# Band scratch laid out with four heads side by side, and a new table of step times, in a two-thread fused kernel

## The reference, cut to what matters

```
for l in 0..3:
    xn = layernorm(x);  s = attn_l(xn);  g = silu(ffn_l(xn));  x = x + s * g
```

```
weights = softmax(logits over 32 offsets)            # [b, head, t, offset]
out[b, head, t, :] = sum_o weights[b, head, t, o] * value[b, head, t - 31 + o, :]
```

## Time and profile before

| | us |
|---|---|
| median of 3 executions | 3785.52 (3783.11 to 3786.83) |
| the profiled execution | 3781.06 |
| its span, first to last instruction | 3779.3 |
| TensorE busy | 3062.2 (81% of the span) |
| VectorE busy | 2423.9 (64%) |
| ScalarE busy | 1666.3 (44%) |
| GpSimd busy | 597.1 (16%) |
| mean granted TensorE clock | 0.884 of full speed |

### The profile page before, as it was taken

The page is one execution under the profiler, slowest core; times in us unless marked ns, Lnnn a source line. Parts: engine busy times, 40 slices in busy tenths (PEclk is TensorE's granted clock), DMA queues, the critical chain, the costliest instruction groups (busy, mean ns, idle before and its releaser), DMA issues.

```text
span 3779.3 us, 43414 instructions
## 1 busy us (share of the span) xinstructions
PE 3062.2 (81%) x15958; PEld 1536.6 (41%) x16050; DVE 2423.9 (64%) x4577; ACT 1666.3 (44%) x2467; POOL 597.1 (16%) x425
## 2 busy tenths in 40 slices
PE   5468869997799868998589976998679986898579
PEld 1124423553245432554235532454325542355225
DVE  7435876568756775668755686557765687552635
ACT  5314615464245534456154652456344561542143
POOL 2001101311023010321013110230103210130113
PEclk7568869998799979998899987999799987998799
DMA  3530275312842066502753028420565127531344
GB/s 114 62 111 9 53 137 135 104 26 74 141 145 69 21 112 131 151 28 53 136 135 104 24 73 143 144 72 20 111 119 161 32 51 139 131 105 36 75 131 126
DMA packets 331157, 353.80 MB, mean 94 GB/s; under 512 B 98433, under 2 KB 264129, under 8 KB 329345
## 3 DMA queue, kind: packets, MB, share of 16 engines
q1 hardware_dynamic: 330945, 351.02, 40.2%
HBM read 301.70 MB, written 48.61 MB: 93 GB/s over the span
## 4 chain that ended last, share of the span: by engine, by line
PE 52%; DVE 28%; DMA 6%; ACT 5%; issue 5%; POOL 2%; SPq 2%; ACTq 0%; DVEq 0%; POOLq 0%
DVE MX L1613 7%; PE PS L1824 6%; PE PS L1847 6%; PE PS L1851 5%; PE PS L1678 5%; PE PS L1686 5%; PE PS L1111 3%; DVE U L897 3%; PE PS L1792 3%; DMA UU<-k_scratch 3%; DVE U L904 3%; PE PS L1803 2%; DVE D L1667 2%; DVE D L956 1%; POOL D L1419 1%
## 5 line engine op out<-in xcount | busy, mean ns | idle before, releaser
L1419 POOL TENSOR_TENSOR D<-D,GW 128x512 f32<-128x512 f32 x320 | 435.1, 1361 | 1412.6 <-ACT D L1492 1177.5
L787 ACT ACTIVATE U<-U 128x2048 f32<-128x2048 f32 x256 | 487.9, 1909 | 180.5 <-DVE U L897 98.4
L1662 DVE SCALAR_TENSOR_TENSOR D<-D,PS 128x512 f32<-128x512 f32 x336 | 229.0, 681 | 402.3 <-ACT D L1496 284.6
L1492 ACT ACTIVATE D<-PS 128x512 f32<-128x512 f32 x336 | 200.0, 595 | 614.8 <-PE PS L1847 614.8
L1824 PEld LDWEIGHTS PS<-WST,D 128*128 128x128 f32 (+1 forms) x2688 | 354.6, 199 | 165.3 <-DVE D L1667 95.5
L1824 PE MATMUL PS<-WST,D 128*128 128x128 f32 (+1 forms) x2688 | 381.9, 287 | 30.5 <-DVE D L1667 30.5
L1851 PE MATMUL PS<-XT,WST 128*128 128x512 f32 (+1 forms) x672 | 373.3, 638 | 27.4 <-DVE D L1662 26.0
L904 DVE SCALAR_TENSOR_TENSOR U<-PP,RD,QB 128x512 f32<-128x512 f32 x512 | 361.8, 772 | 47.5 <-ACT QB L784 28.7
L1111 PE MATMUL PS<-U,resident 128*32 128x512 f32 x2048 | 303.7, 673 | 102.5 <-ACT U L787 102.5
L1847 PE MATMUL PS<-XT,WST 128*128 128x512 f32 (+1 forms) x672 | 370.2, 634 | 8.5 <-DMA WST<-in_pairs_dram 4.3
L1613 DVE TENSOR_REDUCE MX<-PS 128x2 f32<-128x1024 f32 x256 | 297.9, 1219 | 88.1 <-PE PS L1770 88.1
(11 more groups left out here) (356 smaller groups left out, 3822.0 us busy)
## 6 DMA issues: line engine op xcount, KB each, us to landing
GW<-gates_scratch SPq DMA_DIRECT2D x320, 256.0 KB, 4.4
WST<-in_pairs_dram SPq DMA_DIRECT2D x336, 192.0 KB, 2.4
U<-band_scratch SPq DMA_DIRECT2D x32, 1280.0 KB, 15.3
UU<-in_w_dram SPq DMA_DIRECT2D x64, 512.0 KB, 7.2
UU<-pad_scratch SPq DMA_DIRECT2D x8, 1792.0 KB
UU<-q_scratch SPq DMA_DIRECT2D x24, 384.0 KB
UU<-k_scratch SPq DMA_DIRECT2D x24, 384.0 KB
e_scratch<-D SPq DMA_DIRECT2D x8, 1024.0 KB, 4.5
```

The source lines that it names most:

```text
L787: e.activation(ring(i), ring(i), ACT.Gelu).then_inc(S["act"], 1)
L1419: e.tensor_tensor(AV[:, n % 3, :], AV[:, n % 3, :], GW[:, p // 2 % GWS, p % 2, :], ALU.mult).then_inc(S["gated"], 1)
```

## The change

It has two parts.

**Layout.** `band_scratch` becomes `(NT, NH/4, P, 4*BAND)`: the bands of four heads lie interleaved, element by element, in one matrix of 640 columns. A store's run is 32 offsets of 4 heads (128 floats, 512 bytes), a load's run is 640 floats (2560 bytes), four per partition where 16 were. The bytes are the same. `WBT` takes the same order, so ScalarE's copy L803 becomes two activations of half the size (one per half of the heads). L1164 reads a head's band at a step of four floats.

```diff
-        z_dram = nc.dram_tensor("band_scratch", (NT, NH, P, BAND), FP32).ap()
+        z_dram = nc.dram_tensor("band_scratch", (NT, NH // 4, P, 4 * BAND), FP32).ap()
...
-                dst = bass.AP(z_dram.tensor, j * NH * P * BAND, [[BAND + 1, P], [P * BAND, NH], [1, HOR]])
-                e.dma_start(dst, WBT[:, j, :, :]).then_inc(S[f"z_stored{j}"], 16)
+                dst = bass.AP(z_dram.tensor, j * NH * P * BAND, [[4 * BAND + 4, P], [4 * P * BAND, NH // 4], [1, 4 * HOR]])
+                e.dma_start(dst, WBT[:, j].rearrange("p g o r -> p g (o r)")).then_inc(S[f"z_stored{j}"], 16)
...
-                e.dma_start(band(j), z_dram[j].rearrange("n p t -> p n t")).then_inc(S[f"band{j}"], 16)
+                e.dma_start(band(j).rearrange("p g t r -> p g (t r)"), z_dram[j].rearrange("g p t -> p g t")).then_inc(S[f"band{j}"], 16)
...
-                src = PS(j).rearrange("p (h o n) -> p h n o", h=2, o=HOR)
-                e.activation(WBT[:, j, :, :].rearrange("p (h n) o -> p h n o", h=2), src, ACT.Copy).then_inc(S["soft_act"], 1)
+                for h in range(2):
+                    src = PS(j)[:, 256 * h:256 * h + 256].rearrange("p (o g r) -> p g o r", o=HOR, g=2)
+                    last = e.activation(WBT[:, j, 2 * h:2 * h + 2], src, ACT.Copy)
+                last.then_inc(S["soft_act"], 1)
...
-                                            band(j)[:, 8 * h + 2 * q + r, 0:w], start=(j == 0 and r == 0),
+                                            band(j)[:, 2 * h + q // 2, 0:w, 2 * (q % 2) + r], start=(j == 0 and r == 0),
```

**Table.** All ten rows of `STARTS` have new numbers; `TURN` stays 428.30. Of two of them:

```diff
     "a_pool": (
-        1.68, 20.45, 281.18,
+        -133.071, -114.235, 30.902,
     ),
```

More of the change, by code:

```diff
@@ L176 @@
     "a_act": (
[8 rows of a table removed]
[8 rows of a table added]
     ),
     "a_dve": (
[9 rows of a table removed]
[9 rows of a table added]
     ),
     "a_pe": (
[11 rows of a table removed]
[11 rows of a table added]
     ),
     "a_pool": (
-        1.68, 20.45, 281.18,
+        -133.071, -114.235, 30.902,
     ),
     "a_sp": (
-        -64.99, 194.30, 199.03, 213.93, 216.90, 219.88, 222.86, 230.96, 236.26, 241.56, 246.86, 263.68, 293.20, 295.65, 297.45, 303.49,
-        307.14, 357.17,
+        -285.656, 254.015, 254.015, 279.712, 283.628, 283.628, 283.628, 283.628, 283.628, 287.920, 287.920, 312.370, 322.639, 325.522, 325.522, 328.546,
+        349.473, 409.374,
     ),
     "b_act": (
[13 rows of a table removed]
[13 rows of a table added]
     ),
     "b_dve": (
[14 rows of a table removed]
[14 rows of a table added]
     ),
     "b_pe": (
[23 rows of a table removed]
[23 rows of a table added]
     ),
     "b_pool": (
[3 rows of a table removed]
[3 rows of a table added]
     ),
     "b_sp": (
[6 rows of a table removed]
[6 rows of a table added]
     ),
@@ L400, in build @@
         ring = lambda i: U[:, (i % RING) * 4 * T:(i % RING + 1) * 4 * T]
-        band = lambda j: U[:, (j % 3) * NH * BAND:(j % 3 + 1) * NH * BAND].rearrange("p (n t) -> p n t", n=NH)
+        band = lambda j: U[:, (j % 3) * NH * BAND:(j % 3 + 1) * NH * BAND].rearrange("p (g t r) -> p g t r", g=NH // 4, r=4)
         UB = U[:, :].bitcast(BF16)
@@ L411, in build @@
         MM = D[:, 4 * (T + PAD):4 * (T + PAD) + 2 * T].rearrange("p (h t) -> p h t", h=2)
-        WBT = D[:, 0:4 * T].rearrange("p (j n o) -> p j n o", j=NT, n=NH)
+        WBT = D[:, 0:4 * T].rearrange("p (j g o r) -> p j g o r", j=NT, g=NH // 4, r=4)
         RCA = D[:, 4 * T:6 * T].rearrange("p (h t) -> p h t", h=2)
@@ L510, in sp_prologue @@
             for j in range(NT):
-                e.dma_start(z_dram[j].rearrange("n p t -> p n t"), zeros[:, 0:NH * BAND].rearrange("p (n t) -> p n t", n=NH)).then_inc(S["scratch_zero"], 16)
+                e.dma_start(z_dram[j].rearrange("g p t -> p g t"), zeros[:, 0:NH * BAND].rearrange("p (g t) -> p g t", g=NH // 4)).then_inc(S["scratch_zero"], 16)
             zrow = zeros[0:P - 72, 0:NH * T // 8].bitcast(BF16).unsqueeze(1).broadcast_to([P - 72, 8, NH * T // 4])
```

## The result

The changed kernel takes 3680.6 us (median of 4, 3677.8 to 3681.6), the kernel before 3784.3 beside it: a ratio of 0.9725 [0.9708, 0.9742], 104 us or 2.7% faster.

The account below looks back on a forecast made before the run. It took TensorE as the bound where full (busy 367 of 443 us a turn), VectorE or a DMA elsewhere. Sum: 3781.1 - 18 - 3 + 17 - 7 = 3770, plus 4.5 = 3774 us; range 3738 to 3855.

Parts of the forecast that it names:

- The DMA of the first turn: First turn's band stores and loads: longer runs at today's rate of runs save 18 us, between 0 and 20.
- The strided read: Band matmuls on TensorE: reading at a step of four makes a group 2.42 us, adding 17 us over seven turns.
- Rival 1: Band matmuls: four streams share one read path, a group takes 4.9 us, 3844 us in all; chance 0.28.
- rival 2: Band matmuls: the strided read costs nothing in column tiles, 3755 us in all; chance 0.18.
- rival 3: Band matmuls: the four streams lose concurrency, a group takes 9.7 us, 3995 us in all; chance 0.06.
- The key loads: Key loads opening the scores, other turns: less contention from band stores saves 3 us in all, between 0 and 4.
- ScalarE's copy: Copy L803 split into two of half the size: costs nothing, at worst 0.6 us in the first turn.
- The table: New order of steps, argued mainly from the expert phase: saves 1 us a turn, 7 in all, within 21 either way.
- Rival 4: The new table costs 3 us a turn through late L579 and bunched ring items, 3802 us in all; chance 0.06.

Follow-up runs that it names:

- E2: The kernel before with the new table alone, in the old layout: 3684.6 us, ratio 0.9727 to the kernel before.
- E1: The kernel before with the new layout alone, keeping the old table: 3765.4 us, ratio 0.9938 to the kernel before.
- E3: The changed kernel with band matmuls reading 160 neighbouring columns instead of every fourth, so band sums use other weights: 3663.8 us.
- E10: New layout and old table, with the new order only from the end of thread a's turn to the transposes opening layer 2: 3726.8 us against E1's 3765.4.
- E7: New layout and old table, with the new order only from the end of layer 1's first scores to thread a's turn end: 3733.3 us against E1's 3765.4.
- E11: As E7, but the new order in that stretch on TensorE and ScalarE alone: 3725.8 us, against E1's 3765.4.
- E6: New layout and old table, with the new order only from layer 3's second scores to the end of layer 1's first scores: 3753.8 us against E1's 3765.4.
- E13: E1 with twelve of layer 1's second scores moved later on TensorE alone, each to its next one: 3770.0 us against E1's 3765.4.
- E12: E1 with seven expert-phase ring items moved later on TensorE alone, each right before its next one: 3779.8 us against E1's 3765.4.
- E14: The changed kernel with two heads side by side (3672.7 us alone), plus 15 thread a steps per turn bunched on TensorE alone: 3722.5 us.
- E15: As E14, with 42 steps moved instead of 15: 3737.3 us, against 3672.7 for two heads side by side alone.
- E16: E12 with VectorE's fills and ScalarE's gelus of the ring item four later moved along, six items: 3759.9 us against E12's 3779.8.

## Why the prediction was wrong, point by point

**The DMA of the first turn: right, 18 us forecast, 18.9 measured** (43.5 to 24.6 us). The rate of runs gave 216 GB/s for the stores, measured are 224. With 256 bytes the same rule missed (108 expected, 83 to 92 measured), so part of this hit is luck. The loads, which I left at 311 GB/s, run at about 400. The turn as a whole gained 24.9, and the other 6 us lie outside the round trip: 3.4 ahead of it (the first store leaves at 153.86, not at 157.31), 2.5 behind it. Both go with TensorE's granted clock. Ahead of it, from 120 to 140, it was 0.50 (1.2 GHz) before and in E2, and is 0.59 in the changed kernel and 0.67 in E1; why the layout should do that so early no run tells. At the round trip it was 0.50; now it is 0.63 and 0.77 in the rows above, so partly 2.4 GHz, and the first turn's mean is 0.72 instead of 0.65. The four matmuls L1174 take 1.95 us where L1172 took 3.35:

```profile
201.96 3.35 PE L1172 MATMUL PS<-QE,consts 128*128 128x512 f32 x4 [1.24 <-ACT QE L811]
```
```profile
179.62 1.95 PE L1174 MATMUL PS<-QE,consts 128*128 128x512 f32 x4 [1.24 <-ACT QE L813]
```

The first of these rows is of the kernel before. So a shorter wait can also make what follows it quicker; my upper bound of 20 left that out.

**The strided read: right, 17 us forecast, 17 by E3's median and 17 to 20 by the turns.** A group takes 2.47 us (2.42 forecast), and at the low clock 2.50 (the row at 165.34; granted 0.50 from 164 to 168). The maxima wait 1.29 and 1.00 us. Rival 1 (4.9 us), rival 2 (1.3) and rival 3 (9.7) are refuted.

**The key loads: wrong, but small.** I forecast 0.5 us a turn less. In the chain of waits they take 13.05 to 14.15 us in the seven turns of the kernel before, 13.4 in the mean, and 13.21 to 15.01 in E1, 13.8 in the mean. For the fifth turn E1's row, beside 13.45, is

```profile
1808.77 14.04 DMA UU<-k_scratch
```

So the quicker band stores behind them gave them nothing.

**ScalarE's copy: right.** Two of 0.39 us for one of 0.60, and in the first turn's chain the step from the last transpose to the store is no more than 0.1 us longer.

**The table: wrong, and this is nearly the whole error.** I forecast 7 us and bounded it by 21 either way; measured are 81 us in the seven turns (E1 to after), 94 without the strided read (before to E2). Of the 94 some 9 are the clock at L1278; the 81 hold next to nothing of it. What I said of the one place held: L904 now runs under the down-projections and L1511 follows them, and L605 comes 3.9 us behind the last down-projection (1668.28 to 1672.19) where it came 5.3 behind the earlier trace rows, 1.4 us earlier against 1 forecast. Two steps failed:

- "the items that come later in mid-phase cost nothing while TensorE is full." They gain: in the same full stretch TensorE needs 2 us less, and 1.7 of them are the ring items, which stand in 7 runs and not in 15. The order of that phase and of what follows it gave 39 us (E10). The rows to see it by were there, 8 records in 1.07 us against 24 in 2.78, both in the kernel before.
- The bounds. Ten rows of numbers were new, the steps of every stage moved, and I priced three places of them and took their bounds for the whole. The late stretch (32 to 40 us by E7 and E11) and the scores (12 by E6) stand in no sentence of the prediction. Rival 4 looked at the table only as a risk. The forecast's own upper end, 3797, isn't what its terms' bounds add up to either (3824); here that made no difference. Where within a stretch the new order saves its time is shown for the expert phase; for the scores and the late stretch only that it does, and there the mechanism stays open.

## What to carry to other kernels

When a change carries a new schedule, price it by the whole turn: count for each stage how often the engine that is full changes over, and how long the one that is idle waits, and give the schedule the range of its whole idle time (here 76 us a turn) until a stage rules it out. Move the orders of the engines that feed each other together: bunching TensorE's steps alone gained nothing in E13 and lost 14 to 65 us in E12, E14 and E15, and moving the feeding queues along took E12's loss back (E16). And where a layout trades run length in DRAM against a step in the matmul's operand, try the step at which it still reads at full pace before the longest run.

## What the runs showed of the hardware that I had not expected

- With four column tiles at once, a moving operand in float32 reads at a step of two floats nearly as fast as packed (1.35 us a group against 1.29), and at a step of four in 2.47. At the low clock the step of four costs little: 2.50 us against 2.36 packed.
- The store by bytes per run: 128 bytes 54 GB/s, 256 bytes 83 to 92, 512 bytes 224. That is 422, some 340 and 437 runs a us, so the rate of runs is not quite constant. The Trainium skill's page "DMA: Bandwidth & Descriptors", section "Specifications", gives 512 bytes as the least for line rate. No longer run was stored here, and the loads do not bear it out: 311 GB/s in runs of 640 bytes, some 400 in runs of 2560.
- In a stretch with TensorE full, the time still depends on the order of the same instructions, by 2 us in 88.
- After the same idle time of 3.18 us, the same 16 matmuls took 3.67 us in the kernel before (granted clock 0.50) and 2.15 us in E1 (0.97 from 1584 to 1588).
